# A state-space mixer on one core: the output tile y is summed, gated and transposed in two halves

## The chip, the core and the metric

The kernel runs on one core of a Trainium2 chip. Five engines work beside each other, each through its own list of instructions in order: TensorE (PE, with its weight loads as PEld), VectorE (DVE), ScalarE (ACT), GpSimd (POOL) and SyncE (SP), which starts most of the transfers. They wait for each other on semaphores only. The metric is the device time of the whole program in microseconds (us); lower is better.

## The reference

The input is X, 2 sequences of 1024 tokens with 512 features, in float32. Three layers follow, each with a layer norm before it and a residual sum after it:

```python
x = x + 0.5 * ffn(layernorm(x))      # 8 routed experts, top 2, and a shared one
x = x + mixer(layernorm(x))          # the part that the change touches
x = x + 0.5 * ffn(layernorm(x))
```

The mixer, cut to what matters here (16 heads of 64 features, 1024 in all; state of 128 per head feature):

```python
z, xBC, dt = split(u @ W_in.T)               # xBC then goes through a 4-tap causal conv and silu
x, B, C = split(xBC)
state = exp(dt * A) * state + x * (dt * B)   # token by token
y = C . state + x * D
yg = y * silu(z)
yn = yg * rsqrt(mean(yg * yg) + eps) * norm_w
out = yn @ W_out.T
```

## The kernel before, in words

The plan is `("ffn", "mixer", "ffn")` (PLAN). The mixer works through the sequence in tiles of 128 tokens. There are 16 tiles. A hardware loop over the two sequences (`Fori(0, BATCH)`, one pass is called a turn) holds 8 tiles (TPB); a turn has two blocks (BPB) of four tiles (TB). A block first projects its 512 tokens onto W_in (nine weight units, NWU; conv on DVE, silu on ACT) and then runs the four tiles of the scan, q = 0 to 3.

For a tile n the scan is written in chunked form. On PE, in this order:

- `decays` 0 and 1 (L1922, L1926): exponents of the decay matrix L for four heads each, in banks 0 and 1; ACT takes the exponential (L1003). Products and transposes of x, B and C follow (L1942 to L1947), then `decays` 2.
- `y_features(n - 1)` (L1810 to L1817): the eight 128x128 transposes of the gated y of the tile before, into banks 6 and 7. It starts with a wait on `m_yg`.
- `decays` 3, then `project(n - 1)` (L1831): 24 matmuls with the output weights. They read yT, which ACT (`y_hi`, a copy rounded to fp32r, L753) and DVE (`y_lo`, the rest of it, L1054) write out of banks 6 and 7, half by half.
- `m_C` (L1963, C times the state, banks 6 and 7), the transposes of the next normed tile (L1970), `m_D` (L1977, the new contribution to the state), and last `m_E` (L1985): for each head, L times x, 32 instructions, into bank 6 for heads 0 to 7 and bank 7 for heads 8 to 15. Head groups g = 0 to 3 hold four heads each.

y of tile n is built up in SBUF, in one of two buffers of 128x1024: DVE writes C times state scaled by the decay (L1505, two halves, signal `m_yc`), POOL adds x times D (L729, `m_yd`), DVE adds banks 6 and 7 (L1524 and L1526, one signal `m_yi` after the second), POOL multiplies by silu(z) (L732, one instruction of 128x1024, `m_yg`). Then PE transposes it (above), and ACT sums its squares (L955, `squares`), from which POOL makes the factor rs of the norm (L698 to L700, `rms`). DVE adds the projected tile times rs to X (L1371, `residual`, signal `m_res`).

Where the four tiles of the first block end, `y_features` and `project` of the last tile are put among the projections of the next block (units 0 and 1). Where the turn ends, they stand by themselves after the last `m_E`: `y_features(TPB - 1)`, `project(TPB - 1)`, then waits (`settle`) for all that the turn has started, and the next turn, or the second ffn. In the second ffn, SP's first load of gate weights waits for `m_yg` of tile 14 and the load of up weights for that of tile 15.

The order on every engine is the order in which the code is written; nothing is planned at run time. `after(sem, n, each_turn)` waits until the semaphore has reached n in this turn.

Of the kernel before, what the change touches and what calls it, by code (L numbers as in the profile page):

```python
# [12 lines left out]
NT = TOK // P  # L13
# [96 lines left out]
def program(nc, x, w_router, w_gate, w_up, w_down, w_in, w_dt, conv, heads, norm_w, w_out, out):  # L110
# [356 lines left out]
    with block:  # L467
# [3 lines left out]
        def _(sp):  # L471
# [7 lines left out]
            def ffn(k):  # L479
# [38 lines left out]
                for piece in range(3):  # L518

                    if k and piece < 2:  # L520
                        sp.wait_ge(m_yg, nm * NT - 2 + piece)
                    elif k:
                        wait_residual(sp, k)
                    load(piece, 0)
                    if k == 0 and piece == 1:
                        load_x(1)
# [59 lines left out]
        def _(pool):  # L586
# [84 lines left out]
            def mixer(k):  # L671
# [12 lines left out]
                def turn(i):  # L684
# [17 lines left out]
                    for j in range(BPB):  # L702
                        for u in range(NWU):
                            w = j * NWU + u
                            unit_lo(w + 1)
                            if u == 0 and j:
                                rms(j * TB - 1)
                        for q in range(TB):
                            n = j * TB + q
                            hq = slice(q * HEADS, (q + 1) * HEADS)  # L710
                            pool.wait_ge(l_var, i * TPB + (n + TB + 1))
                            rsqrt_ln(slice(q, q + 1), l_rstd)
                            after(m_dec, j + 1, BPB)
                            after(m_C, n, TPB)
                            after(m_S, n, TPB)
                            pool.wait_ge(m_zero, i + 1)
                            pool.tensor_tensor(S[:, (n + 1) % 2].rearrange("p (h d) -> p h d", d=HD),
                                               S[:, n % 2].rearrange("p (h d) -> p h d", d=HD),
                                               each(dec[:, hq], HD), ALU.mult).then_inc(m_Sd, 1)
                            after(m_xdt, n + 1, TPB)  # L720
                            after(m_D, n, TPB)
                            pool.tensor_tensor(xw[:].rearrange("p (h d) -> p h d", d=HD),
                                               xdt[:].rearrange("p (h d) -> p h d", d=HD),
                                               each(wd[:, hq], HD), ALU.mult).then_inc(m_xw, 1)
                            if q >= 1:
                                rms(n - 1)
                            after(m_yc, n + 1, TPB)
                            after(m_xD, n + 1, TPB)
                            pool.tensor_tensor(y[:, n % 2], y[:, n % 2], xD[:], ALU.add).then_inc(m_yd, 1)  # L729
                            after(m_yi, n + 1, TPB)  # L730
                            after(m_z, 8 * (j + 1), 8 * BPB)
                            pool.tensor_tensor(y[:, n % 2], y[:, n % 2], zs[:, q], ALU.mult).then_inc(m_yg, 1)  # L732
                    rms(TPB - 1)
# [13 lines left out]
        def _(act):  # L747
# [157 lines left out]
            def mixer(k):  # L905
# [10 lines left out]
                def turn(i):  # L916
# [25 lines left out]

                    def y_hi(n):

                        for half in range(2):
                            after(m_F, 2 * n + half + 1, 2 * TPB)
                            after(m_out, n, TPB)
                            split_hi(yT[:, 0, 4 * half:4 * half + 4],
                                     bank[6 + half][:].rearrange("p (c t) -> p c t", c=4), m_yhi)

                    def squares(n):
                        after(m_yg, n + 1, TPB)
                        after(m_rs, n - 1, TPB)
# [3 lines left out]
                    for j in range(BPB):  # L957
                        for u in range(NWU):
# [17 lines left out]
                            else:  # L976
                                if u == 5:
# [3 lines left out]
                                    act.wait_ge(m_wo_lo1, 2)  # L981
                                    after(m_yg, j * TB, TPB)
                                for half in range(2):
# [13 lines left out]
                        for q in range(TB):  # L997
                            n = j * TB + q
                            for g in range(HG):
                                after(m_B, HG * n + g + 1, HG * TPB)  # L1000
                                after(m_E, n, TPB)
                                for h in range(g * GH, (g + 1) * GH):
# [17 lines left out]
                    settle((m_zp, 8 * BPB), (m_conv, BPB * NCH), (m_xc, BPB * NCH),  # L1020
                           (m_yg, TPB), (m_D, TPB), (m_E, TPB), (m_M, HG * TPB), (m_rs, TPB), (m_sq, TPB),
                           (m_out, TPB), (m_yd, TPB))
# [11 lines left out]
        def _(dve):  # L1034
# [314 lines left out]
            def mixer(k):  # L1349
                nf, nm = phase_counts(k)  # L1350
                wait_residual(dve, k)
                def turn(i):
# [21 lines left out]
                    for j in range(BPB):  # L1374
# [78 lines left out]
                        for q in range(TB):  # L1453
# [10 lines left out]
                            for half in range(2):  # L1464
                                hs = slice(half * DI // 2, (half + 1) * DI // 2)
                                after(m_xt, 2 * n + half + 1, 2 * TPB)
                                if half == 0:
                                    after(m_xw, n, TPB)
                                    after(m_E, n, TPB)
                                ins = dve.tensor_tensor(heads_of(xdt[:, hs]), heads_of(bank[4 + half][:]),  # L1470
# [32 lines left out]
                            for half in range(2):  # L1503
# [4 lines left out]
                                if half == 0:  # L1508
# [12 lines left out]

                            after(m_E, n + 1, TPB)
                            after(m_yd, n + 1, TPB)
                            own.mark(dve.tensor_tensor(y[:, n % 2, 0:DI // 2], y[:, n % 2, 0:DI // 2], bank[6][:],  # L1524
                                                       ALU.add))
                            dve.tensor_tensor(y[:, n % 2, DI // 2:DI], y[:, n % 2, DI // 2:DI], bank[7][:], ALU.add)\  # L1526
                                .then_inc(m_yi, 1)
                    y_lo(TPB - 1)
                    residual(TPB - 1)
                    settle((m_xw, TPB), (m_yd, TPB), (m_E, TPB), (m_F, 2 * TPB), (m_sq, TPB), (m_out, TPB),  # L1530
                           (m_yg, TPB), (l_tp, TPB))

# [5 lines left out]
                lo_half(wdt[:, 1], wdt_raw[:], wdt[:, 0], m_wdt_lo)  # L1538
                own_steps = 2 * TB + NCH * (TAPS - 2) + 2 + 21 + 5 + 1 + TB * 5
                with dve.Fori(0, BATCH) as i:  # L1540
# [20 lines left out]
        def _(pe):  # L1561
# [243 lines left out]
            def mixer(k):  # L1805

                def turn(i):
                    after, settle = loop_waits(pe, i)

                    def y_features(n):  # L1810

                        after(m_yg, n + 1, TPB)
                        for half in range(2):
                            for c in range(4):
# [21 lines left out]
                    for j in range(BPB):  # L1836
# [19 lines left out]
                        for u in range(NWU):  # L1856
# [36 lines left out]
                            else:  # L1893
                                if u == CS_UNIT:
                                    decay_sums()
                                for half in range(2):
                                    n = j * 8 + (u - 5) * 2 + half
                                    if u == 5:
                                        wait_residual(pe, k)
                                        after(m_ylo, 2 * j * TB, 2 * TPB)  # L1900
                                        after(m_yi, j * TB, TPB)
                                    else:
# [28 lines left out]
                        for q in range(TB):  # L1931
# [25 lines left out]
                            pe.wait_ge(m_zero, i + 1)  # L1957
                            after(m_yi, n, TPB)
                            after(m_ylo, 2 * n, 2 * TPB)
# [31 lines left out]
                    settle((m_S, TPB), (m_L, HG * TPB), (m_pre, BPB * NCH), (m_res, TPB), (m_ylo, 2 * TPB),  # L1991
                           (m_yi, TPB), (m_Bt, TPB), (m_z, 8 * BPB), (m_dec, BPB), (l_lo, TPB))

# [57 lines left out]
```

## Time and profile before

| What | Value |
|---|---|
| median of 3 runs | 1641.28 us (1639.5 to 1648.27) |
| profiled execution, its own time | 1640.93 us |
| its span, first to last instruction | 1639.2 us |
| busy share of the span | PE 93%, DVE 64%, POOL 49%, ACT 46% |
| mean granted TensorE clock | 0.976 of full |
| mixer, about | 536 to 1115 us of the span |
| the four stretches of scan tiles start about | 601, 740, 894 and 1028 us |
| the two turns end about | 824 and 1114 us |

A line of the timeline has the start in us, the time from the first start to the last end in us, engine, line of the kernel, operation, what is written and read, the form and the number of merged instructions. In square brackets stands the idle time of the engine ahead of it and what ended it. Ends of matmuls are modelled: in a row of matmuls the next group starts about 0.16 us before the modelled end of the one before.

### The profile page before, as it was taken

How to read it: one execution, taken by the hardware profiler on the slowest of the kernel's cores; microseconds unless marked ns; L12 is line 12 of the kernel's file. 1: busy time of each engine (PE TensorE's matmuls, PEld its weight loads, DVE VectorE, ACT ScalarE, POOL GpSimd, SP SyncE). 2: the span in 40 equal slices, each digit the busy share in tenths (PEclk: the TensorE clock that was granted, in tenths of full speed). 3: DMA queues.
4: the chain of work that ended last, by engine and by line, in shares of the span. 5: the costliest groups of instructions: out<-in, count | busy, mean ns of one | idle time of the engine just before them, and what ended most of it. 6: DMA issues, size and time to landing. Idle time of an engine off the chain costs nothing. (4 is left out here: it accounts for less than half of the span.)

```text
span 1639.2 us, 23899 instructions
## 1 busy us (share of the span) xinstructions
PE 1524.5 (93%) x8530; PEld 1294.4 (79%) x8530; DVE 1048.6 (64%) x1739; ACT 750.1 (46%) x1290; POOL 795.7 (49%) x475
## 2 busy tenths in 40 slices
PE   6989999999999989998888899889889999999999
PEld 6767999999877777786667778668668999999877
DVE  7664565666467876687558767765673656566465
ACT  4211666666413653454245346434212666666411
POOL 2111777766444545535524553552111777766442
PEclk9989999999999999999889999997989999999999
DMA  7032677777352110020012002014122778777244
GB/s 287 27 106 63 238 271 265 262 256 273 120 181 78 65 65 1 27 79 12 0 51 68 1 23 69 1 36 148 45 88 79 252 256 280 250 266 280 84 155 128
DMA packets 70872, 214.42 MB, mean 131 GB/s; under 512 B 8096, under 2 KB 8096, under 8 KB 69856
## 3 DMA queue, kind: packets, MB, share of 16 engines
q1 hardware_dynamic: 48672, 155.18, 26.9%
q0 software_dynamic: 11360, 37.23, 7.6%
q10 hardware_dynamic: 10720, 20.45, 3.4%
q8 instruction: 70, 1.15, 0.3%
q14 instruction: 50, 0.41, 0.1%
HBM read 179.80 MB, written 33.03 MB: 130 GB/s over the span
## 5 line engine op out<-in xcount | busy, mean ns | idle before, releaser
L626 POOL TENSOR_TENSOR g_lo<-g_raw,g_hi 128x1408 fp32r<-128x1408 f32 x54 | 179.4, 3322 | 260.9 <-ACT g_hi L753 260.6
L626 POOL TENSOR_TENSOR u_lo<-u_raw,u_hi 128x1408 fp32r<-128x1408 f32 x54 | 174.2, 3226 | 67.8 <-ACT u_hi L753 67.8
L1671 PE MATMUL bank<-u_hi,xgT 128*128 128x352 f32 x624 | 168.5, 333 | 0.0
L1671 PE MATMUL bank<-g_hi,xgT 128*128 128x352 f32 x624 | 162.7, 323 | 0.0
L1694 PE MATMUL bank<-d_hi,hT 128*128 128x512 f32 (+1 forms) x468 | 159.7, 395 | 1.8 <-DVE hT L1054 1.8
L691 POOL TENSOR_TENSOR w_hl<-w_raw,w_hl 128x1024 fp32r<-128x1024 f32 x36 | 88.9, 2470 | 139.9 <-ACT w_hl L753 139.9
L1623 PE MATMUL bank<-xs,g_hi 128*128 128x512 f32 (+1 forms) x384 | 130.4, 422 | 7.5 <-DVE gate L1200 6.6
L1639 PE MATMUL bank<-d_hi,hT 128*128 128x512 f32 (+1 forms) x384 | 126.2, 402 | 5.8 <-DVE hT L1054 3.5
L801 ACT ACTIVATE gate<-bank 128x512 f32<-128x512 f32 (+1 forms) x48 | 28.6, 596 | 222.5 <-PE bank L1623 214.8
L1054 DVE TENSOR_TENSOR hT<-bank,hT 128x384 fp32r<-128x384 f32 x78 | 43.1, 552 | 128.9 <-ACT hT L753 128.9
L1385 DVE SCALAR_TENSOR_TENSOR acc<-pre,cw,acc 128x512 f32<-128x512 f32 x120 | 121.7, 1015 | 4.3
L1209 DVE TENSOR_TENSOR d_lo<-d_raw,d_hi 128x1024 fp32r<-128x1024 f32 x54 | 106.3, 1968 | 27.2 <-ACT d_hi L753 27.2
L1871 PE MATMUL bank<-xs,w_hl 128*128 128x512 f32 x480 | 115.9, 399 | 7.2 <-issue 5.0
L1623 PE MATMUL bank<-xs,u_hi 128*128 128x512 f32 (+1 forms) x384 | 121.5, 397 | 0.0
L668 POOL DMA_INDIRECT yg<-routed_y,slots x64 | 66.9, 1046 | 98.3 <-DVE X L1232 57.4
L1671 PEld LDWEIGHTS bank<-g_hi,xgT 128*128 128x128 f32 x624 | 111.0, 188 | 3.6
L1871 PEld LDWEIGHTS bank<-xs,w_hl 128*128 128x128 f32 x480 | 91.1, 192 | 28.7 <-issue 9.0
L1671 PEld LDWEIGHTS bank<-u_hi,xgT 128*128 128x128 f32 x624 | 110.5, 188 | 0.0
L1908 PE MATMUL bank<-w_hl,xs 128*128 128x256 f32 x768 | 96.7, 287 | 14.3 <-ACT zs L986 10.9
L1054 DVE TENSOR_TENSOR d_lo<-d_raw,d_hi 96x512 fp32r<-96x512 f32 x54 | 109.4, 2027 | 0.0
L1908 PEld LDWEIGHTS bank<-w_hl,xs 128*128 128x128 f32 x768 | 94.3, 195 | 16.8 <-ACT zs L986 11.7
L1694 PEld LDWEIGHTS bank<-d_hi,hT 128*128 128x128 f32 (+1 forms) x468 | 87.9, 188 | 21.2 <-DVE hT L1054 4.7
(255 smaller groups left out, 3688.7 us busy)
## 6 DMA issues: line engine op xcount, KB each, us to landing
g_raw<-in_w_gate SPq DMA_DIRECT2D x54, 704.0 KB, 5.6
u_raw<-in_w_up SPq DMA_DIRECT2D x54, 704.0 KB, 6.5
d_raw<-in_w_down SPq DMA_DIRECT2D x54, 512.0 KB, 5.0
w_raw<-in_w_in SPq DMA_DIRECT2D x37, 512.0 KB, 3.2
routed_y<-ys ACTq DMA_DIRECT2D x32, 512.0 KB, 4.7
d_raw<-in_w_down SPq DMA_DIRECT2D x54, 192.0 KB, 5.4
token_x<-xn SPq DMA_DIRECT2D x8, 1024.0 KB, 5.3
X<-in_x SPq DMA_DIRECT2D x4, 1024.0 KB, 10.3
```

The costliest lines, as they stand in the source:

```text
L626: pool.tensor_tensor(half_of(piece, 1, s), raw_at[piece][s % RING][:], half_of(piece, 0, s).bitcast(F), ALU.subtract)\
L668: pool.indirect_dma_start(yg[:, t % 2, slot], None, routed_y, slot_rows(slot * NT + t))\
L691: pool.tensor_tensor(w_hl[:, w % 2, 1], w_raw[:, w % 2], w_hl[:, w % 2, 0].bitcast(F), ALU.subtract).then_inc(m_wlo, 1)
L1054: dve.tensor_tensor(hl_lo, value, hl_hi.bitcast(F), ALU.subtract).then_inc(signal, 1)
L1209: dve.tensor_tensor(lo[:, 0:2], raw[:, 0:2], hi[:, 0:2].bitcast(F), ALU.subtract)
L1385: ins = dve.scalar_tensor_tensor(acc[:, c % 2], pre[:, c % 2, tap:tap + D], cw[:, c, tap:tap + 1], acc[:, c % 2], ALU.mult, ALU.add)
L1623: ins = pe.matmul(dst[0:fw, 0:width], half_of(part, hw, s)[:, kc, f0:f0 + fw], x_of(hx, kc), start=(n == 0), stop=(n == 3 * KD - 1))
L1639: ins = pe.matmul(bank[4 + a][:], hT[0:fw, hh, c, a * P:(a + 1) * P], half_of(2, hw, s)[0:fw, c], start=(c == 0 and m == 0), stop=(c == NF ...
L1671: ins = pe.matmul(dst[:, 0:FE], xgT[:, n % 2, hx, kc], half_of(piece, hw, NS + j)[:, kc], start=(m == 0), stop=(m == 3 * KD - 1))
L1694: ins = pe.matmul(bank[Y + n % 2][:], hT[0:fw, hh, c, 0:P], half_of(2, hw, NS + j)[0:fw, c], start=(m == 0), stop=(m == 3 * NF - 1))
L1871: ins = pe.matmul(bank[c % 2][:], wt[:, hw, kc, (c % 2) * P:(c % 2 + 1) * P], xb[:, hx, kc], start=(m == 0), stop=(m == 3 * KD - 1))
L1908: ins = pe.matmul(bank[6 + half][:, (q % 2) * WU:(q % 2 + 1) * WU], xb[:, hx, kc, q * P:(q + 1) * P], wt[:, hw, kc], start=(m == 0), stop= ...
```

## The change

The sum of y with banks 6 and 7, the gating and the transposes are signalled in halves of eight heads (512 columns). `m_E`, `m_yi` and `m_yg` count two steps a tile where they counted one, and all waits on them count in twos. PE signals `m_E` after head group 1 and after head group 3. DVE waits for `m_yd` first, then for each half of `m_E`, adds its bank and signals. POOL's multiplication becomes two instructions of 128x512, each with its own wait and signal. PE's `y_features` waits for each half before its four transposes. The order of the instructions on each engine stays; `halves` is a new argument that no call sets.

```diff
 # GpSimd
-                            after(m_yi, n + 1, TPB)
                             after(m_z, 8 * (j + 1), 8 * BPB)
-                            pool.tensor_tensor(y[:, n % 2], y[:, n % 2], zs[:, q], ALU.mult).then_inc(m_yg, 1)
+                            for half in range(2):
+                                hs = slice(half * DI // 2, (half + 1) * DI // 2)
+                                after(m_yi, 2 * n + half + 1, 2 * TPB)
+                                pool.tensor_tensor(y[:, n % 2, hs], y[:, n % 2, hs], zs[:, q, hs], ALU.mult)\
+                                    .then_inc(m_yg, 1)
 # VectorE
-                            after(m_E, n + 1, TPB)
                             after(m_yd, n + 1, TPB)
-                            own.mark(dve.tensor_tensor(y[:, n % 2, 0:DI // 2], y[:, n % 2, 0:DI // 2], bank[6][:],
-                                                       ALU.add))
-                            dve.tensor_tensor(y[:, n % 2, DI // 2:DI], y[:, n % 2, DI // 2:DI], bank[7][:], ALU.add)\
-                                .then_inc(m_yi, 1)
+                            for half in range(2):
+                                hs = slice(half * DI // 2, (half + 1) * DI // 2)
+                                after(m_E, 2 * n + half + 1, 2 * TPB)
+                                dve.tensor_tensor(y[:, n % 2, hs], y[:, n % 2, hs], bank[6 + half][:], ALU.add)\
+                                    .then_inc(m_yi, 1)
 # TensorE
-                    def y_features(n):
-
-                        after(m_yg, n + 1, TPB)
-                        for half in range(2):
+                    def y_features(n, halves=range(2)):
+
+                        for half in halves:
+                            after(m_yg, 2 * n + half + 1, 2 * TPB)
                             for c in range(4):
                                 ins = pe.transpose(bank[6 + half][:, c * P:(c + 1) * P],
                                                    y[:, n % 2, (4 * half + c) * P:(4 * half + c + 1) * P], ident[:])
...
                                 for h in range(g * GH, (g + 1) * GH):
                                     ins = pe.matmul(bank[6 + h // 8][:, (h % 8) * HD:(h % 8 + 1) * HD], L[:, h],
                                                     xdt[:, h * HD:(h + 1) * HD], start=True, stop=True)
-                            ins.then_inc(m_E, 1)
+                                if g % 2:
+                                    ins.then_inc(m_E, 1)
 # SyncE, second ffn
-                        sp.wait_ge(m_yg, nm * NT - 2 + piece)
+                        sp.wait_ge(m_yg, 2 * (nm * NT - 2 + piece))
```

## Rows read from the trace of the kernel before

**Rows 1.** PE over the mixer: stretch, length, busy (count), granted clock, DMA share, GB/s

```profile
536.00:1115.00 579.00, 514.89 (x3097) 0.97 0.10 35
```

**Rows 2.** PE's waits over the whole span: us in total, times, longest

```profile
PE bank L1815 <- POOL y L732: 22.6, 14, 3.8
PE bank L1831 <- DVE yT L1054: 8.6, 14, 0.6
```

**Rows 3.** Timeline of PE, first to third tile of the first block

```profile
612.19 3.68 PE L1985 MATMUL bank<-xdt,L 128*128 128x64 f32 x32
...
618.07 0.39 PE L1926 MATMUL bank<-cs_rows,head_row 96*128 96x128 bf16 x4
619.77 1.09 PE L1815 MATMUL bank<-ident,y 128*128 128x128 f32 x8 [1.31 <-POOL y L732]
...
621.93 5.71 PE L1831 MATMUL bank<-wo,yT 128*128 128x512 f32 x24 [0.63 <-DVE yT L1054]
...
638.83 1.09 PE L1815 MATMUL bank<-ident,y 128*128 128x128 f32 x8 [1.22 <-POOL y L732]
```

**Rows 4.** Timeline of DVE in the same tile

```profile
615.91 0.69 DVE L1524 TENSOR_TENSOR y<-y,bank 128x512 f32<-128x512 f32 x1 [2.23 <-PE bank L1985]
616.52 0.68 DVE L1526 TENSOR_TENSOR y<-y,bank 128x512 f32<-128x512 f32 x1
...
618.31 1.29 DVE L1470 TENSOR_TENSOR xdt<-bank,dts 128x512 f32<-128x512 f32 x2
621.09 1.29 DVE L1054 TENSOR_TENSOR yT<-bank,yT 128x512 fp32r<-128x512 f32 x2 [1.49 <-ACT yT L753]
```

**Rows 5.** Timeline of POOL in the same tile

```profile
611.61 2.36 POOL L729 TENSOR_TENSOR y<-y,xD 128x1024 f32<-128x1024 f32 x1 [3.66 <-DVE y L1505]
617.36 2.35 POOL L732 TENSOR_TENSOR y<-y,zs 128x1024 f32<-128x1024 f32 x1 [3.40 <-DVE y L1526]
```

**Rows 6.** Timeline of ACT in the same tile

```profile
617.63 1.17 ACT L1003 ACTIVATE L<-bank,ncs 128x128 f32<-128x128 f32 x4
620.46 1.09 ACT L753 ACTIVATE yT<-bank 128x512 fp32r<-128x512 f32 x2 [1.65 <-PE bank L1815]
```

**Rows 7.** POOL by form: of the page (128x1408), of the mixer (128x1024, 128x1); busy, mean ns

```profile
L626 POOL TENSOR_TENSOR u_lo<-u_raw,u_hi 128x1408 fp32r<-128x1408 f32 x54 | 174.2, 3226 | 67.8 <-ACT u_hi L753 67.8
...
L732 POOL TENSOR_TENSOR y<-y,zs 128x1024 f32<-128x1024 f32 x16 | 37.7, 2356 | 51.8 <-DVE y L1526 51.8
...
L614 POOL TENSOR_TENSOR rstd<-rstd,eps 128x1 f32<-128x1 f32 x16 | 3.0, 189 | 9.2 <-DVE rstd L1046 9.2
```

**Rows 8.** Timeline of PE at the end of the second turn

```profile
1095.72 3.68 PE L1985 MATMUL bank<-xdt,L 128*128 128x64 f32 x32
1103.19 1.97 PE L1815 MATMUL bank<-ident,y 128*128 128x128 f32 x8 [3.80 <-POOL y L732]
1105.72 8.30 PE L1831 MATMUL bank<-wo,yT 128*128 128x512 f32 x24 [0.56 <-DVE yT L1054]
```

**Rows 9.** Timeline of DVE at the same place

```profile
1099.43 0.69 DVE L1524 TENSOR_TENSOR y<-y,bank 128x512 f32<-128x512 f32 x1 [2.23 <-PE bank L1985]
...
1114.06 0.75 DVE L1371 SCALAR_TENSOR_TENSOR X<-bank,rs,X 128x512 f32 x1 [7.54 <-PE bank L1831]
```

**Rows 10.** Granted clock there: stretch, length, PE busy (count), clock

```profile
1101.00:1102.00 1.00, 0.00 (x0) 0.50 0.00 0
...
1111.00:1112.00 1.00, 1.00 (x5) 0.89 0.00 0
```

**Rows 11.** Clock: first block's first tile (PE); fourth block's tiles (instructions on y)

```profile
606.00:608.00 2.00, 1.76 (x6) 0.51 0.03 8
...
1030.00:1099.00 69.00, 3.28 (x24) 2.57 (x24) 9.00 (x14) 3.65 (x6) 16.49 (x7) 1.00 0.06 22
```

**Rows 12.** Timeline of PE: first tile of the fourth block; first projections of the second turn

```profile
1031.75 0.39 PE L1922 MATMUL bank<-mask_b,ident_b 128*128 128x512 bf16 x1 [1.36 <-ACT L L1003]
...
829.02 13.84 PE L1871 MATMUL bank<-xs,w_hl 128*128 128x512 f32 x48 [5.04 <-issue]
```

More of the change, by code:

```diff
@@ L941, in conv_out, with y_hi @@
                         act.activation(xc[:, c], acc[:, c % 2], ACT.Silu).then_inc(m_xc, 1)
-                    def y_hi(n):
-                        for half in range(2):
+                    def y_hi(n, halves=range(2)):
+                        for half in halves:
                             after(m_F, 2 * n + half + 1, 2 * TPB)
@@ L951, in squares @@
                     def squares(n):
-                        after(m_yg, n + 1, TPB)
+                        after(m_yg, 2 * (n + 1), 2 * TPB)
                         after(m_rs, n - 1, TPB)
@@ L981, in turn @@
                                     act.wait_ge(m_wo_lo1, 2)
-                                    after(m_yg, j * TB, TPB)
+                                    after(m_yg, 2 * j * TB, 2 * TPB)
                                 for half in range(2):
@@ L1000, in turn @@
                                 after(m_B, HG * n + g + 1, HG * TPB)
-                                after(m_E, n, TPB)
+                                after(m_E, 2 * n, 2 * TPB)
                                 for h in range(g * GH, (g + 1) * GH):
@@ L1020, in turn @@
                     settle((m_zp, 8 * BPB), (m_conv, BPB * NCH), (m_xc, BPB * NCH),
-                           (m_yg, TPB), (m_D, TPB), (m_E, TPB), (m_M, HG * TPB), (m_rs, TPB), (m_sq, TPB),
+                           (m_yg, 2 * TPB), (m_D, TPB), (m_E, 2 * TPB), (m_M, HG * TPB), (m_rs, TPB), (m_sq, TPB),
                            (m_out, TPB), (m_yd, TPB))
@@ L1468, in turn @@
                                     after(m_xw, n, TPB)
-                                    after(m_E, n, TPB)
+                                    after(m_E, 2 * n, 2 * TPB)
                                 ins = dve.tensor_tensor(heads_of(xdt[:, hs]), heads_of(bank[4 + half][:]),
@@ L1520, in turn @@
                             dve.tensor_tensor(new[:, DI // 2:DI], new[:, DI // 2:DI], bank[5][:], ALU.add).then_inc(m_S, 1)
-                            after(m_E, n + 1, TPB)
                             after(m_yd, n + 1, TPB)
-                            own.mark(dve.tensor_tensor(y[:, n % 2, 0:DI // 2], y[:, n % 2, 0:DI // 2], bank[6][:],
-                                                       ALU.add))
-                            dve.tensor_tensor(y[:, n % 2, DI // 2:DI], y[:, n % 2, DI // 2:DI], bank[7][:], ALU.add)\
-                                .then_inc(m_yi, 1)
+                            for half in range(2):
[3 more added lines that the diff above has]
+                                    .then_inc(m_yi, 1)
                     y_lo(TPB - 1)
                     residual(TPB - 1)
-                    settle((m_xw, TPB), (m_yd, TPB), (m_E, TPB), (m_F, 2 * TPB), (m_sq, TPB), (m_out, TPB),
-                           (m_yg, TPB), (l_tp, TPB))
+                    settle((m_xw, TPB), (m_yd, TPB), (m_E, 2 * TPB), (m_F, 2 * TPB), (m_sq, TPB), (m_out, TPB),
+                           (m_yg, 2 * TPB), (l_tp, TPB))
                 for piece in range(2, 4):
@@ L1538, in mixer @@
                 lo_half(wdt[:, 1], wdt_raw[:], wdt[:, 0], m_wdt_lo)
-                own_steps = 2 * TB + NCH * (TAPS - 2) + 2 + 21 + 5 + 1 + TB * 5
+                own_steps = 2 * TB + NCH * (TAPS - 2) + 2 + 21 + 5 + 1 + TB * 4
                 with dve.Fori(0, BATCH) as i:
@@ L1808, in turn @@
                     after, settle = loop_waits(pe, i)
-                    def y_features(n):
-                        after(m_yg, n + 1, TPB)
-                        for half in range(2):
+                    def y_features(n, halves=range(2)):
+                        for half in halves:
+                            after(m_yg, 2 * n + half + 1, 2 * TPB)
                             for c in range(4):
@@ L1900, in turn @@
                                         after(m_ylo, 2 * j * TB, 2 * TPB)
-                                        after(m_yi, j * TB, TPB)
+                                        after(m_yi, 2 * j * TB, 2 * TPB)
                                     else:
@@ L1957, in turn @@
                             pe.wait_ge(m_zero, i + 1)
-                            after(m_yi, n, TPB)
+                            after(m_yi, 2 * n, 2 * TPB)
                             after(m_ylo, 2 * n, 2 * TPB)
@@ L1991, in turn @@
                     settle((m_S, TPB), (m_L, HG * TPB), (m_pre, BPB * NCH), (m_res, TPB), (m_ylo, 2 * TPB),
-                           (m_yi, TPB), (m_Bt, TPB), (m_z, 8 * BPB), (m_dec, BPB), (l_lo, TPB))
+                           (m_yi, 2 * TPB), (m_Bt, TPB), (m_z, 8 * BPB), (m_dec, BPB), (l_lo, TPB))
                 with pe.Fori(0, BATCH) as i:
```

## The prediction

> **What bounds the kernel now.** I read the busy time by stretch first. In the mixer PE is busy 514.89 of 579 us at a granted clock of 0.97 [rows 1], so 64 us of it are idle, and PE can only gain by having fewer or shorter waits, or a higher clock. The list of PE's waits says which: the largest of the whole span is that of the transposes of y (L1815) for POOL's gating (L732), 22.6 us in 14 waits, the longest 3.8 [rows 2]. There are 16 calls of `y_features`. The two that do not wait are those placed among the projections of a turn's second block. That leaves twelve inside tile steps and two at the ends of the turns.
>
> The timeline shows both kinds. In a tile, PE ends the decays at 618.07 + 0.39 = 618.46, then waits 1.31 us and transposes at 619.77; the next tile shows 1.22 [rows 3]. Four of the twelve waits are of the first kind (the tile after a block's first), eight of the second. At the end of a turn nothing else is left for PE: `m_E` ends at 1095.72 + 3.68 = 1099.40 and the transposes start at 1103.19 after 3.80 us [rows 8]. There the clock is lost too. PE stood still from 1099.40, the granted clock is 0.50 in 1101 to 1102, the lower level of 1.2 GHz, and comes back in 1111 to 1112 (0.89 for that us) [rows 10]. The eight transposes take 1.97 us there against 1.09 in a tile, and the 24 matmuls of `project` 8.30 against 5.71 [rows 3, 8].
>
> **The chain that each wait stands for.** In a tile: E ends at 612.19 + 3.68 = 615.87; DVE adds two halves, 615.91 to 616.52 + 0.68 = 617.20; POOL gates, 617.36 to 619.71; PE transposes at 619.77 [rows 3 to 5]. The change lets the first half run ahead of the end of E and halves the POOL step behind the second.
>
> **Tile step, step by step.** The 32 E instructions take 3.68 us, so the first 16 are done at 612.19 + 1.9 = 614.1. POOL's sum with x times D ends at 611.61 + 2.36 = 613.97 [rows 5], just before it. DVE's first half: 614.15 to 614.84, while DVE was idle for the 2.23 us ahead of 615.91 [rows 4]. So that half costs nothing, and nothing is queued behind it that could go earlier. POOL starts some 0.16 later, as at 617.36, at 615.0.
>
> A POOL multiplication of 128x512 isn't in the trace. Lower bound: rows of 1408 and 1024 elements take 3226 and 2356 ns [rows 7], 2.27 ns an element, 36 ns left over, so 1.20 us for 512. Upper bound of the ordinary kind: the 128x1 row of 189 ns taken as fixed [rows 7] leaves 2.12 ns an element, 1.27 us. I take 1.25. The farthest upper bound is 2.36 us, no gain from halving, the whole row again. First half: 615.0 to 616.25. Second half: DVE 615.91 to 616.60, POOL 616.76 to 618.0. PE reaches the transposes at 618.46, less the 0.16 us by which a group follows before the modelled end of the one before, so 618.30, and both halves are there (the second is asked for only half a group later). The wait is gone whole. With 2.36 us per half the second would end at 619.7 and still give about 0.9 us.
>
> [...]
>
> What is late next: behind the transposes stand ACT's copy and DVE's rest, 619.77 to 621.93 for PE, 2.16 us [rows 3]. ACT's exponentials end at 617.63 + 1.17 = 618.80 and the copy would start at 618.30 + 0.69 = 618.99 [rows 6]. DVE's xdt ends at 618.31 + 1.29 = 619.60, and the rest would start at 621.09 - 1.47 = 619.62 [rows 4]. Both fit, by 0.2 and 0.02 us. DVE moreover gains 0.6 us, since only one half is left behind the end of E, and xdt follows it. PE's wait of 0.63 us for the rest [rows 3] stays. So `project` and everything behind it, paced by PE, moves by the same 1.47.
>
> Gain in the tiles: 22.6 - 2 x 3.8 = 15.0 us of waits, and 12 x 0.16 = 1.9 us because the groups then follow without a gap: **16.9 us**.
>
> **End of a turn.** The offsets are those of the tile: first half E at 1097.64, DVE to 1098.37, POOL 1098.5 to 1099.75, PE free at 1099.24, transposes of the first half at 1099.8. Second half: DVE 1099.43 to 1100.12 [rows 9], POOL 1100.2 to 1101.45, transposes at 1101.5. `project` needs the first half of yT, 1099.8 + 2.16 = 1101.96, and PE has issued the second four transposes by about the same moment. It starts at 1102.0 instead of 1105.72, 3.7 us earlier. The second half of yT comes at about 1103.7, hidden behind the first 12 matmuls (2.85 us). What is left of the idle time is 0.5 and 1.2 us, in place of 3.80.
>
> Does the clock stay at 2.4 GHz? Waits of this size stand before the block's first scan tile: 1.36 us ahead of the third decays [rows 12]. In the fourth block, which has them, the clock is 1.00 over all four tiles; in the first block it was 0.51 in 606 to 608 [rows 11]. I count that as one lost in a few. I take it that it stays. Then `project` takes 5.71, ends at 1107.7 instead of 1114.02, and DVE's residual at 1114.06 [rows 9] moves with it: 6.3 us. If it falls all the same, 3.7. Next turn and second ffn start from the residual and the settled waits, their weights are loaded from earlier signals that mean the same tile as before, so the gain stays. Both ends: **12.6 us**.
>
> **Counters.** The doubled waits name the same events. PE's signal in the middle of E and two fewer own-step marks of DVE I cost at nothing: no row shows a signal's price, and PE issues 32 matmuls in 3.68 us with other groups signalling in between. If each middle signal cost as much as one more E instruction, 3.68/32 = 0.115 us, that would be 16 x 0.115 = 1.8 us less gain.
>
> **Sum.** 16.9 + 12.6 = 29.5 us. The profiled execution took 1640.93 us (span 1639.2, 1.7 around it), which gives 1611.4; the median of the runs is 0.35 us above, so 1611.8. I say **1612 us**, 1.8% less.
>
> **Rivals.**
>
> 1. *The clock falls at the ends nevertheless* (or falls in a tile where it did not before). For: the first block lost it near waits of such a size [rows 11, 12]. Against: the fourth block kept it through 1.36 us and through all its tile steps, which have waits like the 1.22 and 0.63 of [rows 3]. Time: 16.9 + 2 x 3.7 = 24.3, 1617 us. 20%.
>
> 2. *The tile step does not give its wait back*: ACT or DVE holds yT up, since DVE's margin is 0.02 us by the old order of times. Then PE's wait at L1831 grows from 0.63 to about 2.1 and only the ends gain, 12.6: 1628 us. Half of that is as possible, 1620. Against: DVE's 0.6 us. 10%.
>
> 3. *Slower*: with PE's waits at other moments, the clock falls inside tile steps. One fall costs what it costs at the end of a turn, (1.97 - 1.09) + (8.30 - 5.71) = 3.5 us [rows 3, 8]. In all twelve steps that is 42, less the 29.5, so 1654 us. It is slower than 0.5% (8.2 us) only from 11 falls in 12. Against: the change takes idle time out of PE and adds none. 3%.
>
> 4. *The change doesn't do what it says*, because the second half alone sets the transposes: it would need a POOL half that takes as long as the whole and DVE late too; then 1635 to 1641. 3%.
>
> 5. *More*: the low clock also goes where it now stands behind other idle time, as in the 48 matmuls after the first turn, 13.84 us [rows 12] against 11.4 for 48 at the 5.71 per 24 of `project`. Some 2.4 there, and as much in the first block. 1606. 6%.
>
> The forecast has the remaining 58%, with 1608 to 1616 as its own range.
>
> **How the numbers follow.** A measurement of this kernel can tell about 0.5% (8.2 us) from no change. The forecast and rivals 1, 2 and 5 are faster than that (94%, of which I leave 1 to the half cases), 4% within it, 3% slower. Low end: rival 5 with 2 us of shifted clock. High end: rival 1 and the half of rival 2, so 1604 to 1623.
>
> **What would show it.** PE's list of waits should lose L1815 <- POOL from 22.6 to about 3 us, all at the ends of the turns. From one tile's transposes to the next one's there should be 17.6 us in place of 638.83 - 619.77 = 19.06 [rows 3]. POOL's L732 should appear as 32 instructions of about 1.25 us, the first of each pair starting before E ends. PE's wait at L1831 should stay at 0.6. At the end of a turn `project` should take 5.7 us at a clock of 1.00. I am wrong if the L1831 waits grow by what L1815 loses (rival 2), if the granted clock in tile steps is below 1.00 (rival 3), or if `project` at the ends still takes over 8 us (rival 1).

## The result and the profile after

The changed kernel takes 1612.68 us (median of 4, 1611.99 to 1616.87) against 1640.8 for the kernel before (median of 4): ratio 0.9835, 95% interval 0.9814 to 0.9856. On two other occasions it was 0.9843 (0.9816 to 0.9869) and 0.9849 (0.9835 to 0.9864). The profiled execution is the slowest of the four, 1616.87, with a span of 1615.1, 24.1 us less than the profiled one before; by the medians the gain is 28.1 us. In one run further down, e11_best, one execution of six took 3823.81 us at a granted clock of 1.00; nothing here explains it, and it stands in no ratio.

PE's waits over the whole span, the lines that answer to [rows 2] (L1818 was L1815, L1834 was L1831; behind the releaser: us in total, times, longest):

```profile
PE bank L1834 <- DVE yT L1057: 7.5, 12, 0.6
...
PE bank L1818 <- POOL y L734: 2.9, 4, 1.1
```

The 22.6 us are 2.9, in four waits: two halves at each of the two ends. In the tile steps none is left, and the wait for yT hasn't grown. The timeline of PE, DVE, POOL and ACT in the tile of [rows 3 to 6]:

```profile
611.99 3.68 PE L1988 MATMUL bank<-xdt,L 128*128 128x64 f32 x32
...
617.86 0.39 PE L1929 MATMUL bank<-cs_rows,head_row 96*128 96x128 bf16 x4
618.09 1.04 PE L1818 MATMUL bank<-ident,y 128*128 128x128 f32 x8
...
620.20 5.69 PE L1834 MATMUL bank<-wo,yT 128*128 128x512 f32 x24 [0.63 <-DVE yT L1057]
```

```profile
613.99 0.69 DVE L1529 TENSOR_TENSOR y<-y,bank 128x512 f32<-128x512 f32 x1 [0.52 <-PE bank L1988]
615.70 0.69 DVE L1529 TENSOR_TENSOR y<-y,bank 128x512 f32<-128x512 f32 x1 [1.03 <-PE bank L1988]
...
619.36 1.29 DVE L1057 TENSOR_TENSOR yT<-bank,yT 128x512 fp32r<-128x512 f32 x2 [0.57 <-ACT yT L756]
```

```profile
614.75 1.26 POOL L734 TENSOR_TENSOR y<-y,zs 128x512 f32<-128x512 f32 x1 [1.00 <-DVE y L1529]
616.47 1.27 POOL L734 TENSOR_TENSOR y<-y,zs 128x512 f32<-128x512 f32 x1 [0.45 <-DVE y L1529]
```

E (the 32 matmuls that signal `m_E`) ends at 615.67; POOL's first half began 0.9 us before that, and its second is over at 617.74, 0.35 us before PE gets to the transposes at 618.09. The next tile's transposes start at 635.70, 17.61 us later; before it was 19.06 [rows 3]. DVE now waits 0.57 us for ACT's copy where the old order of times left it 0.02.

The end of the second turn, which answers to [rows 8, 9], and the granted clock there (stretch, length, PE busy, clock):

```profile
1078.35 3.68 PE L1988 MATMUL bank<-xdt,L 128*128 128x64 f32 x32
1082.44 0.66 PE L1818 MATMUL bank<-ident,y 128*128 128x128 f32 x4 [0.41 <-POOL y L734]
1084.16 1.02 PE L1818 MATMUL bank<-ident,y 128*128 128x128 f32 x4 [1.06 <-POOL y L734]
1084.83 7.07 PE L1834 MATMUL bank<-wo,yT 128*128 128x512 f32 x24
```

```profile
1091.94 0.75 DVE L1374 SCALAR_TENSOR_TENSOR X<-bank,rs,X 128x512 f32 x1 [5.40 <-PE bank L1834]
```

```profile
1083.00:1084.00 1.00, 0.09 (x1) 1.00 0.00 0
1084.00:1085.00 1.00, 0.84 (x5) 0.65 0.00 0
...
1087.00:1088.00 1.00, 1.00 (x4) 0.64 0.00 0
```

The waits are 0.41 and 1.06 us as forecast (0.5 and 1.2), but the clock fell to its lower level from 1084 to 1088, and the projection took 7.07 us, not 5.71. From the start of E to the residual there are 13.59 us, against 1114.06 - 1095.72 = 18.34 before [rows 8, 9]: 4.75 less.

The clock also fell where the first profile before had kept it. PE in the second block's z projections (the matmuls that make the gate z) and first scan tile:

```profile
715.22 13.26 PE L1911 MATMUL bank<-w_hl,xs 128*128 128x256 f32 x96 [2.69 <-ACT zs L989]
...
739.65 0.61 PE L1925 MATMUL bank<-mask_b,ident_b 128*128 128x512 bf16 x1 [0.69 <-ACT L L1006]
```

Before, in the same block:

```profile
720.11 11.78 PE L1908 MATMUL bank<-w_hl,xs 128*128 128x256 f32 x96 [2.70 <-ACT zs L986]
...
743.06 0.39 PE L1922 MATMUL bank<-mask_b,ident_b 128*128 128x512 bf16 x1 [0.69 <-ACT L L1003]
```

The wait of 2.7 us is the same; the 96 matmuls behind it take 1.48 us longer. The account of the two profiled executions, from starts in the timelines:

| Where | us less |
|---|---|
| twelve tile steps, each four E starts of a block (57.30 to 57.42 before, 52.83 after) | 18.2 |
| two ends of turns, E to residual (18.30 and 18.34; 13.59 twice) | 9.5 |
| ahead of the first E, and the second turn's first projections | 0.8 |
| z projections at the lower clock, three blocks, 13.26 against 11.78 | -4.4 |
| first scan tiles at the lower clock, three blocks, 0.76 each | -2.3 |
| sum, and measured to the last residual (1114.06 - 1091.94) | 21.8, 22.1 |
| second ffn, 10.2 us at the lower clock instead of 13.6, and the rest | 2.0 |

### The profile page after: what moved, and what is told of

Same layout as the page of the kernel before. It is cut to its first block and busy times, and to the rows that moved or that the text cites. A ratio compares the mean times of both kernels' runs of the same rounds, so it can differ in the third digit from the quotient of the medians.

```text
span 1615.1 us, 23935 instructions
## 1 busy us (share of the span) xinstructions
PE 1522.0 (94%) x8530; PEld 1294.3 (80%) x8530; DVE 1044.0 (65%) x1739; ACT 750.3 (46%) x1290; POOL 796.0 (49%) x491
## 5 line engine op out<-in xcount | busy, mean ns | idle before, releaser
L1911 PE MATMUL bank<-w_hl,xs 128*128 128x256 f32 x768 | 101.1, 295 | 14.3 <-ACT zs L989 10.9
L1911 PEld LDWEIGHTS bank<-w_hl,xs 128*128 128x128 f32 x768 | 98.7, 203 | 16.8 <-ACT zs L989 11.7
```

The lines of the kernel that those rows point to most:

```text
L1911: ins = pe.matmul(bank[6 + half][:, (q % 2) * WU:(q % 2 + 1) * WU], xb[:, hx, kc, q * P:(q + 1) * P], wt[:, hw, kc], start=(m == 0), stop= ...
```

## The experiments

Each compares with the kernel before on the same chip in the same hour, whose median went from 1637.9 to 1639.1 (e1 to e4 beside each other, e5 to e8, and e9 to e11 on another chip; e12_before_third is a single execution). The ratio is an estimate of its own and not exactly the quotient of the two medians. "End" is the time from the start of the last E of the first turn to the residual in the profile: 18.30 us before, 13.59 changed.

| Run | Edit | us | ratio (95%) | end |
|---|---|---|---|---|
| e1_again | changed kernel | 1613.7 | 0.9843 (0.9816 to 0.9869) | 13.6 |
| e5_again | changed kernel | 1614.0 | 0.9849 (0.9835 to 0.9864) | 13.6 |
| e9_before_again | kernel before | 1638.2 | 1.0013 (0.9992 to 1.0033) | 18.27 |
| e12_before_third | kernel before | 1642.4 | one execution | 18.12 |
| e2_pool_whole | gating whole | 1634.2 | 0.9977 (0.9959 to 0.9996) | 17.32 |
| e3_e_once | E signalled once | 1614.6 | 0.9853 (0.9818 to 0.9887) | 16.23 |
| e6_pe_both | transposes wait for both | 1616.6 | 0.9868 (0.9849 to 0.9886) | 16.12 |
| e4_ends_only | halves at the ends only | 1629.8 | 0.9948 (0.9927 to 0.9969) | 12.01 |
| e7_fill_ends | waits at ends filled | 1610.9 | 0.9820 (0.9807 to 0.9834) | 12.01 |
| e8_fill_all | and in first tiles | 1611.2 | 0.9829 (0.9809 to 0.9849) | 12.0 |
| e10_f0_early | first transposes earlier | 1603.0 | 0.9784 (0.9762 to 0.9807) | 11.98 |
| e11_best | that, and filled ends | 1603.9 | 0.9778 (0.9756 to 0.9799) | 12.0 |

**Which part of the change carries the tile step.** Three runs undo one part each.

```diff
# e2_pool_whole, GpSimd
-                            for half in range(2): ... gate 128x512, wait and signal each
+                            after(m_yi, 2 * n + 2, 2 * TPB)
+                            pool.tensor_tensor(y[:, n % 2], y[:, n % 2], zs[:, q], ALU.mult).then_inc(m_yg, 2)
# e3_e_once, VectorE
-                                after(m_E, 2 * n + half + 1, 2 * TPB)
+                                after(m_E, 2 * n + 2, 2 * TPB)
# e6_pe_both, TensorE
-                            after(m_yg, 2 * n + half + 1, 2 * TPB)
+                            after(m_yg, 2 * n + 2, 2 * TPB)
```

> POOL gates y in one instruction of 128x1024 after both halves of the sum; all other waits stay in halves. Theory: in a tile DVE's second half ends 0.7 us after E, POOL takes 2.36 us, so the transposes start 0.8 us later than in the changed kernel, a wait of about 0.6 us comes back twelve times, 9.5 us; at the two ends 2.6 us each later and the clock lost for all of the projection, some 1.2 us more each, 7.6. Together 1629 us. Rival, that the early E signal and DVE's split alone bring the tile gain: about 1620 or below, with no wait of the transposes in tile steps.

> DVE waits for the whole of E before the first half of its sum, as the kernel before did; DVE, POOL and the transposes stay in halves. Theory: in a tile POOL's first half ends 2.1 us after E, before PE comes to the transposes (2.4 us after), and the second half makes them wait about 0.4 us in their middle, which comes out of the 0.63 us that PE waits for yT anyway, so the tile steps keep all of their gain; at the two ends the projection starts 1.5 us later and runs at the lower clock for longer, 3 to 5 us for both. 1615 to 1618 us. Rival, that the early signal of E's first half carries the tile gain: 0.6 us in each of twelve steps more, 1622 to 1625.

> Only the transposes wait for both halves of the gated y; E, DVE and POOL stay in halves. Theory: in a tile POOL's second half ends 0.3 us before PE comes to the transposes, so PE's split wait brings nothing there and the tile gain stays whole; at the two ends the first transposes and with them the projection start 1.5 us later, and the projection runs longer at the lower clock, up to 1.2 us, so 3 to 5 us in all: 1615 to 1619 us. Rival, that the transposes need their own halves in the tiles: a wait at them in all twelve tile steps and 1622 or more.

With the gating whole, the wait is back in every tile step; PE in the third tile of the first block:

```profile
636.63 1.09 PE L1815 MATMUL bank<-ident,y 128*128 128x128 f32 x8 [0.70 <-POOL y L732]
638.79 5.71 PE L1831 MATMUL bank<-wo,yT 128*128 128x512 f32 x24 [0.63 <-DVE yT L1054]
```

A step takes 636.63 - 618.11 = 18.52 us instead of 17.61, 10.9 us over twelve, and the ends 3.7 and 3.5 more: 18.1. By the medians it is 20.5 us slower than e1, 1634.2 where 1629 was expected; its ten executions lie between 1630.85 and 1638.23, and the profiled one is the fastest, 13.4 above that of e1, with one fall of the clock fewer in the z projections. What is left of the difference isn't settled. Rows and time speak against the rival. But the rival has a part of the truth: against the kernel before, whose step is 19.06, this one is still 0.5 us shorter, and that comes from the early signal and DVE's split.

With E signalled once, the tile step is 17.64 us, and the wait only changes place, into the middle of the transposes, where it eats the 0.63 us for yT:

```profile
613.97 0.61 PE L1818 MATMUL bank<-ident,y 128*128 128x128 f32 x4
615.00 0.66 PE L1818 MATMUL bank<-ident,y 128*128 128x128 f32 x4 [0.42 <-POOL y L734]
...
616.09 5.71 PE L1834 MATMUL bank<-wo,yT 128*128 128x512 f32 x24
```

e6 has no wait at the transposes in tile steps either; its two are at the ends, 2.1 us each, and 1616.6 us is as expected. Both lose 2.5 us and more at an end, yet e3 is only 0.9 us above e1 (1614.6, just under the 1615 to 1618 expected) and e6 2.6 above e5. The profiles have the rest in the clock: e3 lost it in two z projections and no first tile, e1 in three and three, which is 3.8 us at the prices of the table above; e6 in two and one, e5 in three and two, 2.2 us. So once POOL works in two instructions, PE's early signal and its split wait add nothing in the tile step and pay at the ends only. Without the POOL halves the early signal is worth the 0.5 us of e2. DVE's own signal for each half, which the POOL halves need, was not taken out by itself.

**Do the two gains add?**

```diff
# e4_ends_only, VectorE; PE's wait on m_yg in the same way, and POOL gates 128x1024 at once where n < TPB - 1
-                                after(m_E, 2 * n + half + 1, 2 * TPB)
+                                after(m_E, 2 * n + (2 if n < TPB - 1 else half + 1), 2 * TPB)
```

> The halves are used only for the last tile of a turn; in the other seven, DVE waits for all of E, POOL gates 128x1024 at once and the transposes wait for that, as before. Theory, the two gains add: only the ends gain, 4.7 us each at the clock that the changed kernel's profile shows and up to 6.3 if it stays at the full level, so 9.5 to 12.6 below the kernel before, 1628 to 1631 us, and the wait of 1.2 to 1.3 us is back in twelve tile steps. Rival, that the gain of the ends depends on the shifted tiles (or the reverse): a time outside 1626 to 1633.

The twelve waits are back (16.3 us in all), and the time is 8.2 us below the kernel before, within 1628 to 1631. The changed kernel is 24.2 below it in the same hour, 16 more, but this is no clean price of the tile steps, because the clock differs too. From E to E the twelve steps of this profile are 20.7 us longer than those of e1, 1.5 of it because one of them lost the clock; its ends are 3.2 shorter, and it has one loss fewer in the z projections and one in the first tiles (2.2 together). The sum of these is 15.3; the steps alone, at the full clock, are 19.2 apart, since those of e4 are also 0.1 us longer each than those of the kernel before. Its ten executions lie between 1626.73 and 1635.78, the profiled one, 1626.99, at the low end, so the others need not have this pattern. In this profile both ends kept the clock, with the very waits of the changed kernel:

```profile
805.74 0.66 PE L1821 MATMUL bank<-ident,y 128*128 128x128 f32 x4 [0.41 <-POOL y L737]
807.46 0.66 PE L1821 MATMUL bank<-ident,y 128*128 128x128 f32 x4 [1.06 <-POOL y L737]
807.90 5.72 PE L1837 MATMUL bank<-wo,yT 128*128 128x512 f32 x24
```

12.01 us from E to the residual is 6.3 less than before, to the tenth what the prediction had for an end at full clock. The tile step that lost the clock shows it in its projection, behind waits of 1.36 and 0.63 us:

```profile
922.46 7.22 PE L1837 MATMUL bank<-wo,yT 128*128 128x512 f32 x24 [0.63 <-DVE yT L1060]
```

**What the clock costs, and whether idle time loses it.**

```diff
# e7_fill_ends, TensorE, at the end of a turn; fill(b, n) is n matmuls of 128x512 in bf16 into bank b
-                    y_features(TPB - 1)
+                    after(m_L, HG * TPB, HG * TPB)
+                    fill(0, 2)
+                    y_features(TPB - 1, (0,))
+                    fill(0, 5)
+                    y_features(TPB - 1, (1,))
# e8_fill_all, also in the first tile of a block
+                            if q == 0:
...
+                                fill(6, 7)
                             decays(n, q, 2)
                             if q >= 1:
                                 y_features(n - 1)
+                            else:
+                                fill(6, 3)
                             decays(n, q, 3)
```

> The changed kernel again, as the measure for the three kernels beside it on the same chip and for the count of losses of the clock: 1612 to 1614 us, and, if the moment decides, another pattern of first tiles at the lower level than four of four and three of four.

> The changed kernel, with seven extra matmuls of 128x512 in bf16 at each end of a turn, whose product nobody reads: two ahead of the first four transposes and five ahead of the second four, in the time in which PE waits for POOL (0.41 and 1.07 us). Theory A, the clock falls at an end because PE stands idle there: with the waits filled it stays at 1.00 until the projection is over, which then takes 5.7 us and not 7.05, so 1.3 us less at each end, 2.7 in all: 1610 to 1611 where the changed kernel takes 1613. Rival B, that it falls for another reason (the small matmuls of E, or the transposes themselves): the lower level stands at the same place and the time is the same or some tenths longer.

> As the kernel with extra matmuls at the ends, and with ten more in the first tile of each block: seven ahead of the third group of exponents, three ahead of the fourth, where PE waits 1.36 and 0.69 us for ACT. Theory A, idle time of this size is what loses the clock there, in some executions more often than in others: no first tile shows the lower level any more, each loss avoided is worth about 2 us, 2 to 8 us below the kernel filled at the ends only, so 1604 to 1609 us and a smaller spread. Rival B, the losses come from elsewhere or the extra matmuls delay the exponents' matmuls by as much as they save: 1610 or more.

With the waits filled the transposes start at the same distance from E and the projection takes 5.73 us at both ends:

```profile
800.06 0.59 PE L1824 MATMUL bank<-mask_b,ident_b 128*128 128x512 bf16 x2
800.64 0.66 PE L1818 MATMUL bank<-ident,y 128*128 128x128 f32 x4
801.13 1.24 PE L1824 MATMUL bank<-mask_b,ident_b 128*128 128x512 bf16 x5
802.35 0.66 PE L1818 MATMUL bank<-ident,y 128*128 128x128 f32 x4
802.80 5.73 PE L1839 MATMUL bank<-wo,yT 128*128 128x512 f32 x24
```

The median is 3.05 us below e5, for 2.7 expected, and the slowest execution of e7 (1611.91) is below the fastest of e5 (1613.1): theory A is borne out at the ends, in so far as filled waits kept the clock there. They are enough and not always needed, since the unfilled ends of e4 and e10 kept it too. In e8 no first scan tile shows the lower level either, but it brings no time (1611.2 against 1610.9), where 1604 to 1609 was expected. E begins 10.30 us after the first decays (610.69 - 600.39) where e7, which lost the clock there, needs 11.05. So such a loss costs 0.75 us and not the 2 of the expectation, since without it E waits for DVE instead:

```profile
610.69 3.79 PE L2000 MATMUL bank<-xdt,L 128*128 128x64 f32 x32 [0.77 <-DVE y L1508]
```

In every profile this wait of 0.7 to 0.8 us stands before exactly those first E that lost no clock: three times in the first profile before, never in that of the changed kernel.

The Trainium skill, "TensorE: Matmul & The Clock Gate", Part 1, has it that the throttled state is the default and activity releases it. By that rule filling with work whose product nobody reads should hold the clock, and at the ends it does: 5.73 us in place of 7.04.

**Chance of the execution, or of the kernel?**

> The changed kernel itself, once more, for two questions. How far does its time spread, and is the loss of the clock in the first scan tile of all four blocks (its first profile shows the lower level there four times, the kernel before once) a property of the changed kernel? Theory A, the moment decides: the steps are the same and another execution shows another number of such losses, each worth about 2 us; time 1612 us, near the other executions (1612.0 to 1612.7), and fewer than four first tiles at the lower level. Rival B, the shorter steps cause it: four out of four again, and a time of 1612 in spite of it.

> The kernel before itself, for a second profile of it. Theory A: which of its idle times lose the clock outside the ends of the turns is a matter of the moment, so this profile shows low stretches at other places than the first (for instance behind PE's wait of 2.7 us for ACT in a block's z projections, or in the first tile of the second to fourth block), while both ends show the long one of 10 us. Rival B: the kernel before has a fixed pattern, with the one first tile of the first profile, and the changed kernel another, so part of its gain is lost for good to new losses of the clock.

> A third profile of the kernel before, against three of the changed kernel, which all lose the clock behind the wait of 2.7 us for ACT in the z projections of three blocks, and in two to four first tiles. Theory A, the moment of the execution decides: the third profile of the kernel before shows one or more losses at those waits, as the changed kernel's do. Rival B, the pattern belongs to the kernel: none at the z projections of the second to fourth block, as in its first two profiles, one or no first tile, both ends of the turns 10 us at the lower level; time 1636 to 1641 us.

The first two columns count the places that show the lower level:

| Profile | z projections, blocks 2 to 4 | first tiles, blocks 1 to 4 | ends at the lower level, us |
|---|---|---|---|
| before, first | 0 | 1 | 10.2, 10.2 |
| e9_before_again | 0 | 0 | 10.2, 10.2 |
| e12_before_third | 1 | 1 | 10.2, 10.2 |
| after | 3 | 4 | 3.4, 3.4 |
| e1_again | 3 | 3 | 3.4, 3.4 |
| e5_again | 3 | 2 | 3.4, 3.4 |

Neither theory holds alone. The third profile of the kernel before (1642.39 us) does lose the clock once behind the 2.7 us wait, which its first two had kept:

```profile
720.58 13.09 PE L1908 MATMUL bank<-w_hl,xs 128*128 128x256 f32 x96 [2.69 <-ACT zs L986]
```

But 1 of 9 against 9 of 9, in three executions of each, hardly is a chance of single executions: the changed kernel loses it there regularly. The edited kernels lie between (e7 and e8 three of three blocks, e2, e3, e4, e6, e10 and e11 two). In the first block, which the table leaves out, it goes the other way: the kernel before lost the clock in its z projections in three profiles of three, the changed kernel in two. Each costs about 1.5 us, so some 4 us of the gain go to places that the change doesn't touch. What in the new distances in time does it isn't settled by these runs. The spread between executions of one kernel goes with the clock as well: of the eight of e9, the one of 1651.02 us had a mean clock of 0.970, that of 1637.42 one of 0.979.

**A faster one.** The wait of 0.63 us for yT was the last in the tile step. ACT frees it too late, because its copy of G and B comes first.

```diff
# e10_f0_early
 # TensorE
+                            if q >= 1:
+                                y_features(n - 1, (0,))
                             decays(n, q, 2)
                             if q >= 1:
-                                y_features(n - 1)
+                                y_features(n - 1, (1,))
                             decays(n, q, 3)
 # ScalarE, within the exponentials of a tile
-                                if g == 0:
+                                if g == 1 and q >= 1:
+                                    y_hi(n - 1, (0,))
+                                if g == (1 if q else 0):
...
                                     act.activation(GB[:], bank[3][:, 0:2 * P], ACT.Copy).then_inc(m_Bt, 1)
                                 if g == 1 and q >= 1:
-                                    y_hi(n - 1)
+                                    y_hi(n - 1, (1,))
```

> The changed kernel with the first four transposes of y moved ahead of the third group of exponents' matmuls, and ACT's copy of G and B moved behind its copy of the first half of yT. Theory: in a tile ACT is free for yT at 618.45 instead of 618.59 and the first transposes are done before that, so PE's wait of 0.63 us for yT shrinks by 0.25 to 0.3 us in twelve tile steps, 3 to 3.6 us: 1610 to 1611 where the changed kernel takes 1613 to 1614. Rival: DVE, whose xdt ends 0.57 us before it starts on yT, or ACT's second copy, takes over and nothing is gained: 1613 to 1614.

> The earlier first transposes and the extra matmuls at the ends of the turns together, the two edits that should be independent. If the transposes bring 3 us and the filled ends the 3 us that they brought alone: 1607 to 1609 us, 6 below the changed kernel. If only the filled ends count: 1611.

```profile
613.77 0.60 PE L1820 MATMUL bank<-ident,y 128*128 128x128 f32 x4
...
614.65 0.60 PE L1820 MATMUL bank<-ident,y 128*128 128x128 f32 x4
...
615.88 5.72 PE L1836 MATMUL bank<-wo,yT 128*128 128x512 f32 x24 [0.18 <-DVE yT L1059]
```

The wait shrinks from 0.63 to 0.18, more than expected, and a step takes 630.97 - 613.77 = 17.20 us, 0.41 less, and from E to E all twelve are 5.5 us shorter than in e5. The time fell by far more than the 3 to 3.6 us expected, to 1603.0. The changed kernel didn't run beside it, but the two ratios to the kernel before, 0.9784 and 0.9849, are 10.6 us apart. In the profile (span 1600.6 against 1611.4 for e5) the rest is clock: both projections at the ends took 5.69 us, unfilled, with the same waits of 0.41 and 1.06, and the ends are 3.2 us shorter; the fourth block's z projections took 11.77 instead of 13.28, 1.5 us; one first tile more lost the clock, -0.8. That is 9.4 of 10.8. With the ends filled as well nothing is added (1603.9, under the 1607 to 1609 expected as e10 is under its own), as there was no loss left there to avoid. So the margins of small edits here are set by luck with the clock as much as by the steps they save.

## Why the prediction was right

1612 was forecast and 1612.68 measured, and the sign, the place and the mechanism hold. That the two agree within 1 us is luck. The terms were worked out for the profiled execution, and there 24.1 us were gained for 29.5 forecast: the tile steps gave somewhat more, the ends less, and the clock fell at places that had no term. The profiled execution is the slowest of the four, though, 4.2 us above the median, at a granted clock of 0.976 against 0.979 to 0.981 for the others; the forecast meets the median of those, 28.1 below the kernel before, and no trace shows where the others saved it.

- **Tile steps, 16.9 us.** 18.2 measured in the profile. The step went from 19.06 to 17.61; all transposes start without a wait, and `project` keeps its 0.63. Right, with the POOL half at 1.27 us for 1.25 taken.
- **What is late next.** DVE's margin for yT, 0.02 us by the old times plus 0.6, measured 0.57: rival 2 is out.
- **Ends, 12.6 us.** The step that failed is "I take it that it stays": at both ends of the changed kernel the clock fell, in all three profiles. 9.5 us measured. Where it doesn't fall (e4, e7, e10) an end gains the 6.3 us of the prediction. Rival 1 had the right event with too high a price: 3.7 us left of an end, for 4.7 measured, since the low stretch was 3.4 us and not 10.2.
- **Falls elsewhere.** Rival 3 looked for them inside tile steps, at 3.5 us each. In the changed kernel's profiles none came there (in e4's one did, at 1.5 us); they came behind the waits for ACT in the z projections and in first tiles, at 1.5 and 0.76 us, 6.7 us in the profile. The prediction had no term for that. Rival 5 expected the reverse. The second ffn gave about 2 us back.
- **Counters.** PE's signal in the middle of E costs nothing that shows: E takes 3.68 us before and after. The marks of DVE are one fewer a tile, not two as the prediction has it. With the 18.2 and 9.5 in place of 16.9 and 12.6 the steps give 27.7, less 6.7, and about 3 from other places (0.8, 2.0 and 0.3 that the table doesn't place): 24.1.
- **A side sum.** For a POOL half of 2.36 us the prediction says that the tile would still give about 0.9 us. By its own figures the second four transposes would start at 619.7 instead of half a group behind 619.77, at 620.3: 0.6. And with this the 1635 to 1641 of rival 4 follow from no row. Neither is in the forecast, and the half took 1.27.

## What to carry to other kernels

When a long chain crosses engines and one of its members is a slow engine with a whole tile in one instruction, split that instruction and the signals around it, and check for each split whether it is covered: here POOL's was enough by itself in the steady state, with the signal between DVE and POOL that it needs, and the earlier signal of E would have paid only without it. Read the wait that you remove together with the arrival of its queue: a second half that arrives before the queue gets there is free, and a faster first signal then buys nothing. Where a few per mille matter on TensorE, compare the granted clock stretch by stretch before crediting an edit with its time, since falls of the clock at untouched places can take or give several us.

## What the runs showed of the hardware

- A POOL multiplication of 128x512 takes 1.270 us (32 of them, 1.264 to 1.289), of 128x1024 2.356 [rows 7]: 2 x 1.270 - 2.356 = 0.18 us comes on top for each instruction, as the 128x1 row of 0.189 had suggested, and not 0.036.
- The same waits of PE (0.41 and 1.06 us behind E) lost the clock in the changed kernel and kept it in e4 and e10, where they came at other times. A wait of 2.7 us kept it in 8 of 9 blocks of the kernel before (blocks 2 to 4 of three profiles) and lost it in 9 of 9 of the changed one. The length of a wait alone doesn't tell whether the clock falls.
- What a fall of the clock costs depends on how long it lasts and on what PE would wait for otherwise: 10.2 us at the lower level at an end made the projection 8.30 us instead of 5.71, 3.4 us made it 7.07; in a first tile 3.4 us cost 0.75, because E would have waited 0.7 to 0.8 us for DVE anyway (e8 against e7).
